# Second attention's tail in a new order over blocks, and the rotary attention's norm laid out over two tiles

## The reference

```python
def _L2_xattn_ref(x, cond, mask, wq, bq, wk, bk, wv, bv, wo, bo):      # 16 heads of 16
    q = _w8a8_linear(x, wq, bq).reshape(B, N, H, D).transpose(0, 2, 1, 3)
    k = (cond @ wk.T + bk).reshape(B, L, H, D).transpose(0, 2, 1, 3)
    v = (cond @ wv.T + bv).reshape(B, L, H, D).transpose(0, 2, 1, 3)
    attn = jax.nn.softmax(jnp.einsum('bhnd,bhld->bhnl', q, k) * inv_sqrt_d + mask[:, None], axis=-1)
    o = jnp.einsum('bhnl,bhld->bhnd', attn, v).transpose(0, 2, 1, 3).reshape(B, N, C)
    return _w8a8_linear(o, wo, bo)                 # quantises rows of its input and of its weights to 8 bits
...
def _L3_xattn_ref(x, c, Wq, bq, Wk, bk, Wv, bv, Wo, bo):               # 8 heads, rotary positions
    q, k = _apply_rotary(q_emb, q), _apply_rotary(k_emb, k)
    p_attn = jax.nn.softmax(jnp.einsum('bhtc,bhsc->bhts', q, k) / math.sqrt(K_CH), axis=-1)
```

## Time and profile before

| | |
|---|---|
| median of 3 runs | 1494.43 us (1491.14 to 1499.95) |
| profiled execution | 1495.77 us, span 1494.0 us, mean granted TensorE clock 0.938 |
| TensorE busy | 1244.5 us, 83% of the span |
| VectorE busy | 905.8 us, 61% |
| ScalarE busy | 543.0 us, 36% |
| GpSimd busy | 279.8 us, 19% |

### The profile page before, as it was taken

One profiled execution on the slowest core, in us unless ns is written; L12 is line 12 of the kernel. 1 busy time (PEld: TensorE's weight loads), 2 busy tenths in 40 slices (PEclk: granted clock), 3 DMA queues, 4 the chain that ended last, 5 costly groups with the idle time before them and its releaser, 6 DMA issues.

```text
span 1494.0 us, 19944 instructions
## 1 busy us (share of the span) xinstructions
PE 1244.5 (83%) x6750; PEld 697.6 (47%) x6750; DVE 905.8 (61%) x2249; ACT 543.0 (36%) x924; POOL 279.8 (19%) x302
## 2 busy tenths in 40 slices
PE   1127989898979999995888778758999999999998
PEld 0114445444534446663665523324554455456555
DVE  7994454545354336555788768957888888622222
ACT  3373121312111223332566535524554545521110
POOL 1220000000004430003344410144434343000000
PEclk9987999999989999997999958968999999999999
DMA  9200000002000020002111000023222223000000
GB/s 311 68 14 1 0 0 0 0 0 89 0 22 1 0 72 1 0 1 56 43 42 28 1 23 1 1 73 90 84 89 85 86 77 94 12 1 14 14 14 14
DMA packets 70852, 56.90 MB, mean 38 GB/s; under 512 B 26500, under 2 KB 63236, under 8 KB 70532
## 3 DMA queue, kind: packets, MB, share of 16 engines
q1 hardware_dynamic: 70148, 55.81, 12.3%
q10 hardware_dynamic: 640, 0.26, 0.1%
HBM read 41.03 MB, written 14.68 MB: 37 GB/s over the span
## 4 chain that ended last, share of the span: by engine, by line
PE 67%; issue 13%; DVE 11%; POOL 4%; ACT 2%; DMA 1%; DVEq 0%; SPq 0%; POOLq 0%; ACTq 0%
PE banks L1100 7%; PE banks L2335 7%; PE banks L717 6%; PE banks L500 5%; PE banks L496 5%; PE banks L933 4%; PE banks L1107 4%; PE banks L925 3%; PE banks L507 3%; PE banks L511 3%; PE banks L2300 3%; POOL sb_work L1564 2%; PE banks L1807 2%; DVE sb_work L2548 2%; PE banks L2321 1%
## 5 line engine op out<-in xcount | busy, mean ns | idle before, releaser
L2548 DVE TENSOR_REDUCE sb_work<-banks 128x2 f32<-128x512 f32 x256 | 164.6, 685 | 41.0 <-PE banks L2300 38.7
L2440 ACT ACTIVATE sb_work<-banks 128x1024 f32<-128x1024 f32 x128 | 130.9, 1023 | 123.3 <-PE banks L2321 123.2
L617 DVE TENSOR_TENSOR sb_work<-sb_work,banks 128x512 f32<-128x512 f32 x72 | 49.5, 687 | 116.6 <-ACT sb_work L584 116.6
L1100 PE MATMUL banks<-sb_work,sb_shelf 128*128 128x512 f32 x256 | 114.7, 593 | 0.0
L1564 POOL TENSOR_TENSOR sb_work<-sb_work,sb_consts 128x512 f32<-128x512 f32 x64 | 66.2, 1064 | 224.2 <-ACT sb_work L1504 202.8
L584 ACT ACTIVATE sb_work<-banks 128x512 f32<-128x512 f32 x72 | 42.9, 596 | 169.9 <-PE banks L496 109.4
L717 PE MATMUL banks<-sb_work,sb_ctx_nat 128*64 128x512 f32 (+15 forms) x512 | 90.0, 510 | 7.8 <-DVE sb_work L779 7.8
L500 PE MATMUL banks<-sb_work,sb_shelf 128*128 128x512 f32 (+1 forms) x192 | 85.7, 632 | 10.2 <-DVE sb_work L660 8.6
L1179 DVE TENSOR_TENSOR sb_work<-sb_work,banks 128x512 f32<-128x512 f32 x32 | 22.0, 687 | 115.9 <-ACT sb_work L1165 115.9
L1076 POOL TENSOR_TENSOR sb_late<-sb_w2n 128x1024 f32<-128x1024 f32 x10 | 22.7, 2269 | 353.0 <-DVE sb_work L771 352.4
L496 PE MATMUL banks<-sb_work,sb_shelf 128*128 128x512 f32 (+1 forms) x192 | 78.1, 594 | 0.0
(11 more groups left out here) (302 smaller groups left out, 2388.5 us busy)
## 6 DMA issues: line engine op xcount, KB each, us to landing
scratch<-sb_raw SPq DMA_DIRECT2D x32, 192.0 KB, 2.0
sb_raw<-scratch SPq DMA_DIRECT2D x32, 192.0 KB
sb_work<-scratch SPq DMA_DIRECT2D x32, 192.0 KB
sb_work<-ctx_t SPq DMA_DIRECT2D x8, 512.0 KB, 3.5
sb_work<-ctx_t SPq DMA_DIRECT2D x16, 256.0 KB, 4.3
scratch<-sb_raw SPq DMA_DIRECT2D x32, 128.0 KB, 1.9
sb_ctx_nat<-ctx SPq DMA_DIRECT2D x1, 2048.0 KB, 10.8
sb_raw<-wguT SPq DMA_DIRECT2D x1, 2048.0 KB, 15.2
```

Of the source, the lines that this page charges most:

```text
L1100: ins = nc.tensor.matmul(bank[2 * (m % 2) + half], w[:, c, m * P:(m + 1) * P], xT3[:, c, :], start=c == 0, stop=c == KC - 1)
L2440: nc.scalar.activation(pt3[:, h % 2, :, :], o, ACT.Exp).then_inc(exp3, 1)
L2548: nc.vector.tensor_reduce(out=mx3[:, tc, k, 2 * hp:2 * hp + 2], in_=bank[u % 2].rearrange("p (h s) -> p h s", h=2), axis=AX, op=ALU.max).t ...
```

## The change

In the second attention the tail of a block is put in another order. On TensorE the next block's query integers are turned between the transpose and the weighing of tile 3; the queries come before the second half of the keys; then the queries are turned, and the next block's first values and first scores are made, all ahead of the turning of the output's integers and the output product. ScalarE copies keys and queries before the output's integers and takes the next block's first exponentials at the end of the block. VectorE does the next block's first shift and values between the quantising of the output and its scaled output; the norm's statistics come at the head of a block and its steps in tiles 0 and 1, with the application after tile 1; the quantising of the next queries stands ahead of the division of tile 2, the scaled queries ahead of the quantising of the output. The banks are dealt anew: keys 1 and 0 (the very first 1 and 6), query integers 0, queries 2 and 3, turned queries 4 and 5, output 4 and 5. TensorE waits for the update of x before the first transpose of a block's weights, behind the scores of tile 1, instead of ahead of them.

In the rotary attention the norm of the next block goes from three places in tile 1 to 14 places in tiles 0 and 1.

```diff
             def block_(b, last):                                     # attn2_tensor
-                values(b, 0)
-                pe.wait_ge(qT2_ready, b + 1)
-                scores(b, 0)
-                pe.wait_ge(x_done, updated(ph, b))
                 for t in range(BT):
                     if t + 1 < BT:
                         scores(b, t + 1)
                     elif not last:
-                        pe.wait_ge(sc_read, BT * b + 3)
-                        keys(b + 1, 0)
+                        keys(b + 1, 0, KEY_BANKS)
+                    if t == 0:
+                        pe.wait_ge(x_done, updated(ph, b))
                     turn_weights(b, t)
                     if t + 1 < BT:
                         values(b, t + 1)
+                    elif not last:
+                        query_ints(b + 1)
                     weigh(b, t)
                 if not last:
-                    query_ints(b + 1)
-                    keys(b + 1, 1)
+                    pe.wait_ge(sc_read, BT * b + BT)
                     queries(b + 1)
+                    keys(b + 1, 1, KEY_BANKS)
+                    turn_queries(b + 1)
+                    values(b + 1, 0)
+                    pe.wait_ge(qT2_ready, b + 2)
+                    scores(b + 1, 0)
                 pe.wait_ge(o_int_ready, b + 1)
                 turn_ints(o_int, 6).then_inc(o_int_turned, 1)
-                if not last:
-                    turn_queries(b + 1)
                 pe.wait_ge(o_intT_ready, b + 1)
                 by_weights(o_intT, woT2, OUT2_BANKS).then_inc(out2_done, 1)
...
                 if not last:                                         # attn2_scalar, end of a block
                     query_ints(b + 1)
-                    keys(b + 1)
+                    keys(b + 1, KEY_BANKS)
+                    queries(b + 1)
                 ints(b, o_int_turned, o_intT, 6, o_intT_ready)
                 if not last:
-                    queries(b + 1)
+                    exps(b + 1, 0)
...
             def block_(b, last):                                     # attn2_vector
-                shifted_scores(b, 0)
-                own_values(b, 0)
+                link.mark(tile_statistics((b + 1) % BLOCKS))
                 for t in range(BT):
-                    step = {1: 0, 2: 5}.get(t)
+                    step = {0: 0, 1: 5}.get(t)
                     if t + 1 < BT:
                         shifted_scores(b, t + 1, step)
                         own_values(b, t + 1, None if step is None else step + 2)
+                    if t == 2 and not last:
+                        query_ints(b + 1)
                     second(b, t, None if step is None else step + 4)
-                    if t == 0:
-                        link.mark(tile_statistics((b + 1) % BLOCKS))
-                    elif t == 2:
+                    if t == 1:
                         norm_step(link, 10)
                         link.hold()
                         normalise(link, (b + 1) % BLOCKS, step=2)
-                        if not last:
-                            query_ints(b + 1)
+                if not last:
+                    queries(b + 1)
                 dve.wait_ge(o2_ready, BT * b + BT)
                 quantise(link, o_mid, o_mid, o_int, 1.0 / 127.0, 1e-8).then_inc(o_int_ready, 1)
                 if not last:
-                    queries(b + 1)
+                    shifted_scores(b + 1, 0)
+                    own_values(b + 1, 0)
                 dve.wait_ge(out2_done, b + 1)
                 link(scaled(o_mid, OUT2_BANKS, qs, so_b))
...
+            def spread_norm(b, slot):                                # attn3_vector
+                nxt = (b + 1) % BLOCKS
+                if slot < 2:
+                    for t in (2 * slot, 2 * slot + 1):
+                        ins = nc.vector.bn_stats(st[:, t, :], x[:, BT * nxt + t, :])
+                    if slot == 1:
+                        link.mark(ins)
+                elif slot < 9:
+                    norm_step(link, slot - 2)
+                elif slot == 9:
+                    for i in range(7, NORM_STEPS):
+                        norm_step(link, i)
+                elif slot < 14:
+                    t = slot - 10
+                    if t == 0:
+                        link.hold()
+                        dve.wait_ge(p3_q, BT * b + BT)
+                    ins = nc.vector.tensor_scalar(xn[:, t, :], x[:, BT * nxt + t, :], mv[:, t, 0:1], rs[:, t:t + 1],
+                                                  ALU.subtract, ALU.mult)
+                    if t == BT - 1:
+                        ins.then_inc(xn_ready, 1)
...
-                    if t == 1 and h in (1, 3, 5):
-                        if h == 1:
-                            dve.wait_ge(p3_q, BT * b + BT)
-                        normalise(link, (b + 1) % BLOCKS, h // 2)
+                    if t < 2:
+                        spread_norm(b, H3 * t + h)
```

33 lines of the change are left out of this document (19 added, 14 removed).

## The result

| | before | after |
|---|---|---|
| median | 1495.49 us (4 runs, 1491.14 to 1499.95) | 1477.02 us (4 runs, 1471.52 to 1480.07) |
| ratio | | 0.987, 95% interval [0.983, 0.992] |
| profiled execution, its span, mean clock | 1495.77, 1494.0, 0.938 | 1479.34, 1477.5, 0.948 |

What follows compares the result with a forecast made beforehand. TensorE was taken as near full, VectorE not far behind, with block transitions a chain and the rotary norm on VectorE delaying TensorE. -12.5 + 3.7 = -8.8 us against the 1494.4 median gave 1485.5 us; range 1476 to 1496.

Steps and rivals of the forecast that it cites:

- Part 1: Rotary attention: spreading the next block's norm over 14 heads gains 12.5 us, bounds 8 and 15.
- the term for GpSimd's splitting: Rotary attention: small norm pieces slowed beside GpSimd's splitting, allowed 0 to 1.5 us a block, taken as 0.1.
- The step on the odd heads: Rotary attention: norm pieces cost time because behind odd heads VectorE's next division or rotation is what TensorE waits for.
- Part 2: Second attention: new order of tail and norm costs 3.7 us in all, bounds -2 and +9.
- The fourth term: Second attention's tail: rounding of the output's integers falls on GpSimd's masking, 0.4 us a transition, bounds 0 and 1.4.
- a bound of 1.7 us: Second attention: a low stretch of TensorE's clock behind a transition costs up to 1.7 us; one more or less allowed.
- rival (a): Both attentions: pipeline pays, collisions cost nothing, a low clock stretch falls away; attention -4, norm -12.5, 1478 us; chance 0.22.
- what would show it: Signs: rotary first and second tiles 18 to 19 us; second attention's blocks 41 to 42, tail 13.9, second exponentials some 8 behind.
- the step on VectorE's order: Second attention, block start: VectorE's work before tile 1's shift puts second exponentials 7.9 us behind the first, before 6.1.
- the 0.5 us for the update of x: Second attention: update of x falls on GpSimd's addition of the bias, 0.5 us a transition, bounds 0 and 1.0.
- Rival (b): Second attention: VectorE and GpSimd collide as in the upper bounds, +8; Part 1 gives 9; 1493 us; chance 0.27.
- Rival (c): Rotary attention: each small piece waits for a GpSimd instruction, some nine a block; 1520 us at 1.0 us each; chance 0.05.

Runs made afterwards that it cites:

- second set: The kernel after, unchanged, run six more times beside the kernel before: 1479.45 us beside 1492.76, ratio 0.991 [0.989, 0.993].
- e2_norm: Kernel before with only the rotary attention's norm spread over 14 heads, second attention as before: 1481.84 us, ratio to before 0.991 [0.988, 0.994].
- e9_delay: Kernel after plus two VectorE writes to an unused buffer ahead of the second attention: 1479.12 us, ratio to before 0.991 [0.989, 0.993].
- e6_out: Kernel after, but TensorE's first transposes of a block wait only for the reading of banks 4 and 5: 1482.45 us, ratio to before 0.990.
- e12_ahead4: Kernel after with rotary norm at even heads, transposes awaiting only banks 4 and 5, second tile's scores and shift before the update of x: 1479.93 us.
- e8_again: The kernel after itself, unchanged, run again for a second trace: 1479.45 us, ratio to before 0.991 [0.989, 0.993].
- e3_late: Kernel after with second attention's norm and query quantising back in their old places, query integers turned after the last weighing: 1482.74 us, ratio to before 0.992.

## Why the prediction was right, and where not

The time lay in the range, 1 us inside its lower end (3 us in the second set), and the sign was right; but it lay below the forecast's own band of 1482 to 1489, and the gain was half as large again, or twice as large, depending on the set of runs. That it was so much is in good part luck, as the steps show. (Two slips of the sum: 1494.4 less 8.8 is 1485.6, and five sevenths of the band, not four fifths, lie below 1487. Neither changes the reading.) By its steps:

**Part 1** was right in its sum and right by compensation. Forecast 12.5 us, measured 12.0 in e2_norm (300.0 to 288.0) and 11.1 in after, whose first tile took 1.2 us longer than before (38.3 and 37.1; in other kernels it is anything from 36.6 to 39.4 us). In the two middle blocks it is 3.3 and 3.5 us, forecast 3.4. But the term for GpSimd's splitting, 0.1 us a block, was mis-sized: VectorE's busy time grew by 1.2 us, near the upper bound of 1.5. So the pieces must hide better than I gave them, which I infer from the sum and haven't measured. The step on the odd heads was weak: laid to the even heads the norm costs 2 us less in all, not 4 to 7. What the spreading brought was mainly that the work lies in two tiles, each with room for some, and less its exact place.

**Part 2** failed in its sum, +3.7 against -0.7. The order of events was as forecast: 13.5 us of tail (13.9), masking last, 7.7 us to the second exponentials (7.9) with the wait on VectorE, 26.6 us from first exponential to last weighing (27.0). Cut at the first exponentials of the blocks, the sum had -0.8, +1.2, +1.2 and +2.1 (the last one up to the update of x), and measured were -2.9, -0.4, -0.5 and +3.0.

A block in the middle came out 1.7 us below the forecast, and three terms share that. The update of x was to lose 0.5 us to GpSimd's addition of the bias; it began as that addition ended (787.44 in the timeline of the kernel after, the addition from 785.17 for 2.37) and took 1.23 us as before. The tail was 0.8 shorter than its 13.9 + 0.4: the masking began 5.9 us behind the start of the weighing, not 6.2, and the scores ended 5.3 behind that, not 5.5, with some rounding of mine on top. And from first exponential to last weighing it was 26.6 us instead of 27.5 (27.0 with the 0.5 of the update), so 0.4 too much stood there. The fourth term, 0.4 us for the rounding, came out right in size and wrong in its way. All five rounding instructions were stretched, in full. But it was VectorE that was held, 3.7 us of it a block, and not the masking, and VectorE had all but 0.4 us of that time, since the shift behind the rounding waits for the masking anyhow (the scores end at 821.9, the rounding at 822.4). I had read from 4.46 against 4.05 us that GpSimd pays; that was a row in which VectorE had begun first. The Trainium skill, "SBUF — State Buffer", section "Who interferes with whom", was right that each of these instructions excludes GpSimd's (0.35 us alone, 1.13 beside the masking); that the sum would be 4 us worse was my own conclusion from it, and wrong, since most of the held time was slack and the update of x was not held.

What the sum left to its bounds is the clock. Before, the first transition fell into a stretch at 0.84 and 0.73 and took 41.8 us; with the change the clock stays at 1.00 from 701 to 850 us. Table by stretches of the kernel before, its first transition:

```profile
735.00:739.00 4.00, 2.17 (x17) 1.94 (x18) 2.37 (x6) 1.21 (x2) 3.73 (x4) 0.84 0.39 131
739.00:743.00 4.00, 4.00 (x19) 2.96 (x19) 1.92 (x5) 2.55 (x3) 0.73 (x1) 0.73 0.00 0
```

I had this as a bound of 1.7 us and as part of rival (a), and that is the size it has: this transition took 17.2 us from weighing to exponential before, the two behind it 15.5 and 15.4, and block 0 was 2.9 us shorter, blocks 1 and 2 only 0.4 and 0.5. The last block is 3.0 longer: 2.0 up to its last weighing (26.0 for 24.0 us), 1.0 behind it, since the clock falls at 850.7 and the weighing that begins at 850.2 takes 2.86 instead of 1.85 us. The blocks took 39.0, 40.1 and 40.1 us, not the 41 to 42 of "what would show it"; the step on VectorE's order was not refuted by this (the 7.7 us are there); the 0.5 us for the update of x were.

**The stage in between** wasn't in the sum at all. It gave 4.8 us, the largest part of what was missing. It can't be credited to the change: in e9_delay, with the same work and order under another course of the clock, 4.2 of them were gone.

**The chances.** Rival (a), 1478 us with a chance of 0.22, named the time, and its mechanism in part: collisions that cost little and a low stretch of the clock that falls away. That the attention itself would win 4 us was not so; the time came out as (a) had it because of the stage in between. Rival (b) had the stretching of the rounding in full right, its price wrong, and a collision of the update of x that VectorE did not pay. Rival (c) needed 0.3 us for each of nine meetings a block. Measured, three steps met the splitting, at 0.23 to 0.39 us each, and VectorE's busy time grew by 1.2 us a block in all.

## What to carry to other kernels

Where VectorE's short instructions came into a masking of GpSimd's that was already running, it was VectorE that was held. Ask which of the two begins first and whether the one held has slack there before the collision gets a price, and look for it in the busy time of a block rather than in the wait lists. An order that lets GpSimd start sooner can be the slower one, if what it then meets is a chain of small steps on a full VectorE (0.9 us a block in e6_out, 1.2 in e12_ahead4). And a difference of a few microseconds, in a stage whose code was not touched or between two orders, is to be laid beside the clock's falls in both traces before it is put down to a change: one fall of 3.4 us cost a tail of this kernel 1.7.

## What the hardware showed that I had not expected

VectorE's four rounding instructions of 128x256 took 0.35 us each alone and 1.13 beside back-to-back masking on GpSimd, about one masking (1.09) each, when the masking had begun first. GpSimd's eight took 8.7 us, 0.2 more than in two separate halves before. Where VectorE had begun first, with the update of x at 787.44 us, the four maskings from 787.50 on took 5.07 us; in the kernel before four took 4.05.

The low stretch of TensorE's clock behind the second attention lasted 38 to 48 us in the twelve traces without filling: 41 us in after and e8_again, 48 in e9_delay, which has the same work. The clock's return 8 us later into the stage cost its first block only 2.5, nearly all of it in the one wait of 2.4 us shown above. Keeping TensorE busy through the gap held the clock up for another 34 us (to 885.0 instead of 850.7) and brought 0.9 us; then it fell elsewhere, at a worse place.

The stages ahead of the second attention, the same code in all these kernels, ended between 698.6 us (e9_delay) and 705.2 us (e3_late). This spread is nearly half of what the change brings, and the 1487 to 1504 us of the kernel before over its runs are as wide as all of it. It is not explained here.
